# Four fused conv blocks on one core: image 0's input loaded once, late weights spread out, and two residual tiles of the last layer summed by GpSimd

## The chip, the core and the metric

The kernel runs on one core of a Trainium2 chip. The metric is the time of one execution on the device in microseconds (us). The engines are TensorE (PE; PEld is its weight load), VectorE (DVE), ScalarE (ACT), GpSimd (POOL), and SyncE (SP), which here only issues DMAs. Each engine works through its own queue in order and waits on semaphores.

## What is computed

Four images of 512 channels and 32 x 32 pixels go through four blocks, all in float32.

```python
# L0: 1x1 conv to 128, offsets by a 3x3 conv, deformable 3x3 conv, 1x1 conv to 512, residual
mid = relu(bn1(conv1x1(x)));  off = conv3x3(mid) + off_b
y = relu(bn2(einsum(w2, bilinear_gather(mid, off))))
x = relu(bn3(conv1x1(y)) + x)
# L1: correlation with the 5x5 neighbours, normalised, appended to the channels, 1x1 conv to 512
gs = l2norm(stack([sum_c(shift(x, dy, dx) * x) for dy, dx in 5x5]))
x = relu(einsum(W, concat([x, gs])) + b)
# L2, L3: 1x1 conv to 128, 3x3 conv, 1x1 conv to 512, residual
for layer in (2, 3):
    h = relu(s1 * conv1x1(x) + b1);  h = relu(s2 * conv3x3(h) + b2)
    x = relu(s3 * conv1x1(h) + b3 + x)
```

## The kernel before, in words

**The order.** `ORDER` (lines 44 to 200) is one list of some 1,550 items such as `ex.0.3.1.2`: kind, image, and further indices, mostly layer, half `h` of the pixels (512 columns each) and tile `m` of 128 channels. Each engine walks this list and carries out the items that are its own, so the list fixes every queue. It mixes the deformable conv of one image with L1 to L3 of the image before it. Five PSUM banks and a ring of four slots (`assign`, lines 246 to 269) are given out along the list; `take` (line 634) waits until the bank's last user has given it back.

**Start.** SP loads image 0's x into `xa` in eight parts of 256 KB (line 513), then seven weights (lines 514 to 517). ScalarE loads `w1` and the parameters `prm` (lines 828, 829), both counted by `ld_first`. PE runs three warm-up products on zeros (L653), waits for `ld_first` and runs conv1 (L666). ScalarE turns it into `mid`, PE makes the offset taps (L684), transposes (L674) and shifts (L694, L700), and VectorE computes the indices (`index`, L1071 to L1086). ScalarE writes image 0's pixels as a table to DRAM (`write_table`, L499, L501); later tables and the x of images 1 to 3 (`xload`, L507) are SP's.

**Gathers.** An image has 18 units (2 halves x 9 taps) of four gathers, 288 in all. GpSimd issues each as an indirect DMA (L597) and adds a small `tick` behind it (L602); in images 1 to 3 two memsets of `pause` follow each unit (L607). The gathers fill a ring of 12 slots; GpSimd waits for the blend of three units before. ScalarE weighs the first corner (`weigh`, L911), VectorE blends the other three (`blend`, L1189), PE transposes (`turn`, L730), ScalarE copies (`sampT`, L919), PE multiplies (`tap`, L741). After nine taps follow `hid`, `out0` (L749) and the residual sum `xsum` (L1194) with the tile of x that `res` loads into `x1` (L544). A value goes to PE as a high and a low part (fp32r); a product is then three matmuls (L630 to L632).

**The residual of L2 and L3.** It is added in one of two ways. Mostly PE adds it: `ex` starts with two matmuls of the identity with the high and low part of `xs` (L818), and then `exval` (layer 2) or `final` (layer 3: ScalarE at h = 0, L1007; VectorE at h = 1, L1257) applies bias and ReLU. Where `kept_sum` says so (before, only in image 3), GpSimd adds the two parts (`keep`, L613) into `kept`, which lies where `xs_low` lies, as soon as `red` has read them, `ex` is the three product matmuls alone, VectorE adds bank, bias and `kept` (`exsum` or `add`, L1250), and ScalarE applies ReLU (L1002).

The two ways stand in these lines:

```python
                elif kind == "ex":
                    _, i, layer, h, m = it
                    pe.wait_ge(cv_low, nth(("cvlow", i, layer, h)))
                    ...
                    alone = kept_sum(i, layer, m)
                    for p in range(0 if alone else 2):
                        pe.matmul(ps[:], ident_r[:], xs[p][:, m, h * HALF:(h + 1) * HALF], start=p == 0, stop=False)
```

Of the kernel before, what the change touches and what calls it, by code (L numbers as in the profile page):

```python
# [44 lines left out]
conv1.0.0 conv1.0.1 mid.0.0 taps.0.0 mid.0.1 taps.0.2 tapped.0.0 taps.0.1 tapped.0.2 midT.0.0 tapped.0.1 midT.0.1  # L45
pixels.0.0 shift.0 pixels.0.1 table.0.0 table.0.1 scale.0 scale.1 index.0 gather.0.0.0 hats.0 turnw.0 positions.0
turnw.1 split.1 gather.0.0.1 split.4 split.3 split.5 gather.0.1.0 weigh.0.0.0 splitlow.5 blend.0.0.0 gather.0.1.1
weigh.0.0.1 w3turn conv1.1.1 blend.0.0.1 xload.1.0 gather.0.2.0 weigh.0.1.0 gather.0.2.1 turn.0.0 xload.2.1 w3scale
gather.0.3.0 split.2 mid.1.1 split.0 splitlow.0 weigh.0.1.1 sampT.0.0 blend.0.1.0 conv1.1.0 gather.0.3.1 weigh.0.2.0
weigh.0.2.1 blend.0.1.1 gather.0.4.0 tap.0.0 mid.1.0 xload.2.0 midT.1.1 taps.1.1 taps.1.2 splitlow.1 midT.1.0  # L50
weigh.0.3.0 gather.0.4.1 blend.0.2.0 conv1.2.1 weigh.0.3.1 pixels.1.1 splitlow.3 splitlow.4 blend.0.2.1 gather.0.5.0
blend.0.3.0 xload.3.1 turn.0.1 sampT.0.1 tapped.1.1 tap.0.1 blend.0.3.1 gather.0.5.1 weigh.0.4.0 turn.0.2 taps.1.0
bias sampT.0.2 blend.0.4.0 conv1.2.0 tapped.1.2 mid.2.1 tapped.1.0 weigh.0.4.1 gather.0.6.0 blend.0.4.1 weigh.0.5.0
shift.1 gather.0.6.1 blend.0.5.0 mid.2.0 weigh.0.5.1 split.6 blend.0.5.1 gather.0.7.0 w3back turn.0.4 pixels.1.0 w3s
turn.0.3 index.1 midT.2.1 sampT.0.3 xload.3.0 gather.0.7.1 tap.0.2 pixels.2.1 weigh.0.6.0 taps.2.2 midT.2.0 turn.0.5
taps.2.1 corrw blend.0.6.0 splitlow.2 taps.2.0 gather.0.8.0 table.1.0 table.1.1 tap.0.3 sampT.0.5 weigh.0.6.1
pixels.2.0 conv1.3.1 res.0.0.1 blend.0.6.1 weigh.0.7.0 gather.0.8.1 tapped.2.0 weigh.0.7.1 blend.0.7.0 res.0.0.2
table.2.1 res.0.0.3 res.0.0.0 mid.3.1 gather.0.9.0 conv1.3.0 blend.0.7.1 sampT.0.4 weigh.0.8.0 gather.0.9.1 tap.0.4
turn.0.7 splitlow.6 blend.0.8.0 mid.3.0 tapped.2.1 weigh.0.8.1 midT.3.1 tap.0.5 gather.0.10.0 blend.0.8.1 midT.3.0
turn.0.6 pixels.3.0 sampT.0.6 tap.0.6 taps.3.1 weigh.0.9.0 turn.0.8 tapped.2.2 blend.0.9.0 gather.0.10.1 shift.2  # L60
weigh.0.9.1 hats.1 gather.0.11.0 sampT.0.8 blend.0.9.1 positions.1 sampT.0.7 weigh.0.10.0 tap.0.7 gather.0.11.1
tap.0.8 weigh.0.10.1 blend.0.10.0 index.2 gather.0.12.0 hid.0.0 blend.0.10.1 weigh.0.11.0 out0.0.0.0 out0.0.0.3
gather.0.12.1 blend.0.11.0 turn.0.9 weigh.0.11.1 hats.2 out0.0.0.2 sampT.0.9 pixels.3.1 xsum.0.0.0 res.0.1.0 table.3.1
blend.0.11.1 turn.0.11 taps.3.2 gather.0.13.0 weigh.0.12.0 turn.0.10 tapped.3.1 table.2.0 res.0.1.2 xsum.0.0.3
# [1247 lines left out]
```

## Time and profile before

| | us |
|---|---|
| median of 3 runs | 602.6 (602.46 to 603.48) |
| the profiled execution | 605.4 |
| its span | 603.6 |
| PE busy | 562.2 (93%) |
| POOL busy | 409.5 (68%) |
| DVE busy | 442.3 (73%) |
| ACT busy | 327.3 (54%) |

The page cuts the span into 40 slices of 15.1 us; a digit is the busy share of an engine in a slice in tenths. Lines of the profile name the engine, the line of the kernel, what is written from what, and how often. A chain of waits is followed back from the last instruction: at each step to what released it.

### The profile page before, as it was taken

The page shows a single profiled execution, that of the slowest core. Times are in us where ns is not written, and L with a number is a line of the kernel's source. Part 1 is how long each engine was busy: PE and PEld are TensorE (multiplying, and loading weights), DVE is VectorE, ACT ScalarE, POOL GpSimd, SP SyncE. Part 2 cuts the span into 40 slices and gives each one's busy share as a digit, 9 for nine tenths or more (in the row PEclk, how much of TensorE's full clock was granted, in tenths as well). Part 3 has the DMA queues.
Part 4 walks back from the last instruction along what each step waited for, and adds up shares of the span by engine and source line. Part 5 has one row for each costly group of instructions (what it writes and reads, how often), then busy time and mean ns, then how long its engine had stood idle before and what let it go on. Part 6 is the DMA issues. An engine that isn't in the chain of part 4 may idle for free.

```text
span 603.6 us, 8850 instructions
## 1 busy us (share of the span) xinstructions
PE 562.2 (93%) x2550; PEld 416.9 (69%) x2550; DVE 442.3 (73%) x1277; ACT 327.3 (54%) x718; POOL 409.5 (68%) x718
## 2 busy tenths in 40 slices
PE   9478986699999999799999999999999999999996
PEld 4434753576777777469777777688777776987774
DVE  3447789798988788689986788998884674463444
ACT  3445756446654874555645857654557633433534
POOL 2388888888888898888888888888787300003060
PEclk9888998899999999899999999999999999999999
DMA  8898997964568555866586557856765213000003
GB/s 307 286 355 292 276 366 222 310 186 143 160 193 296 165 150 162 280 205 171 168 264 204 168 168 251 251 159 175 223 183 148 72 59 134 0 1 1 1 1 139
DMA packets 48034, 110.08 MB, mean 182 GB/s; under 512 B 7655, under 2 KB 15911, under 8 KB 47858
## 3 DMA queue, kind: packets, MB, share of 16 engines
q0 software_dynamic: 23040, 75.52, 41.8%
q1 hardware_dynamic: 22274, 32.59, 15.6%
q10 hardware_dynamic: 2672, 1.41, 0.8%
q8 instruction: 21, 0.34, 0.3%
q14 instruction: 27, 0.22, 0.1%
HBM read 96.94 MB, written 12.55 MB: 181 GB/s over the span
## 4 chain that ended last, share of the span: by engine, by line
PE 71%; POOL 18%; DVE 4%; issue 3%; DMA 2%; ACT 1%; POOLq 0%; DVEq 0%; ACTq 0%
PE bank L630 16%; PE bank L632 16%; PE bank L631 16%; POOL patch L597 14%; PE bank L741 7%; POOL tick L602 4%; PE bank L749 4%; PE bank L818 4%; PE bank L730 4%; DMA patch<-patch_tables,idx_all 2%; PE bank L787 1%; PE bank L666 1%; PE bank L653 1%; DVE samp L1189 1%; DVE ring L1250 1%
## 5 line engine op out<-in xcount | busy, mean ns | idle before, releaser
L1189 DVE SCALAR_TENSOR_TENSOR samp<-patch,wgt_all,samp 128x128 f32<-128x128 f32 x864 | 240.7, 347 | 22.7 <-ACT samp L911 20.1
L597 POOL DMA_INDIRECT patch<-patch_tables,idx_all x216 | 219.8, 1017 | 40.2 <-DVE samp L1189 10.7
L911 ACT ACTIVATE samp<-patch,wgt_all 128x128 f32<-128x128 f32 x288 | 102.0, 396 | 76.4 <-DMA patch<-patch_table,idx_all 35.3
L597 POOL DMA_INDIRECT patch<-patch_table,idx_all x72 | 70.5, 980 | 30.9 <-DVE far L1086 20.3
L613 POOL TENSOR_TENSOR kept<-xs_high,xs_low 128x512 f32<-128x512 f32 x12 | 16.5, 1405 | 100.3 <-PE bank L632 100.3
L602 POOL TENSOR_TENSOR tick<-tick 1x1 f32<-1x1 f32 x288 | 79.7, 277 | 5.0
L741 PE MATMUL bank<-sampT,w 128*128 128x512 f32 x144 | 71.9, 606 | 1.5 <-ACT sampT L919 1.5
L730 PEld LDWEIGHTS bank<-ident_r,samp 128*128 128x128 f32 x288 | 35.8, 144 | 31.4 <-DVE samp L1189 16.8
L919 ACT ACTIVATE sampT<-bank 128x512 f32<-128x512 f32 x72 | 41.9, 591 | 27.8 <-PE bank L730 26.8
L730 PE MATMUL bank<-ident_r,samp 128*128 128x128 f32 x288 | 44.1, 280 | 10.5 <-DVE samp L1189 10.5
L630 PE MATMUL bank<-x_high,l1w_high 128*128 128x512 f32 x128 | 53.9, 421 | 0.0
L632 PE MATMUL bank<-x_high,l1w_low 128*128 128x512 f32 x128 | 50.2, 392 | 0.0
L631 PE MATMUL bank<-x_low,l1w_high 128*128 128x512 f32 x128 | 50.0, 391 | 0.0
L741 PEld LDWEIGHTS bank<-sampT,w 128*128 128x128 f32 x144 | 25.5, 193 | 17.4 <-issue 11.5
L630 PE MATMUL bank<-x_high 128*128 128x256 f32 x128 | 37.5, 293 | 0.0
L1230 DVE TENSOR_TENSOR h_low<-ring,h_high 128x512 fp32r<-128x512 f32 x16 | 12.1, 756 | 34.6 <-ACT h_high L983 34.6
L632 PE MATMUL bank<-x_high,x_low 128*128 128x256 f32 x128 | 36.2, 283 | 0.0
L631 PE MATMUL bank<-x_low,x_high 128*128 128x256 f32 x128 | 36.2, 283 | 0.0
L943 ACT ACTIVATE corr<-bank 32x320 f32<-32x320 f32 x64 | 27.3, 427 | 16.3 <-PE bank L632 14.0
L666 PE MATMUL bank<-xa,w 128*128 128x512 f32 x64 | 32.1, 651 | 2.6 <-DMA xa<-in_x 2.6
L749 PE MATMUL bank<-hid,w 128*128 128x512 f32 x64 | 31.7, 616 | 1.8 <-issue 1.8
L630 PE MATMUL bank<-hp_high,l2w_high 128*128 128x512 f32 x72 | 30.1, 418 | 0.0
(187 smaller groups left out, 1203.1 us busy)
## 6 DMA issues: line engine op xcount, KB each, us to landing
x_whole<-in_x SPq DMA_DIRECT2D x32, 256.0 KB, 7.2
out_y<-ring SPq DMA_DIRECT2D x32, 256.0 KB, 3.3
xa<-in_x SPq DMA_DIRECT2D x6, 1024.0 KB, 8.5
patch<-patch_tables,idx_all POOLq DMA_INDIRECT x216, 3.5
patch_tables<-midT SPq DMA_DIRECT2D x11, 256.0 KB, 7.1
xa<-in_x SPq DMA_DIRECT2D x8, 256.0 KB, 5.7
patch<-patch_table,idx_all POOLq DMA_INDIRECT x72, 6.0
l1w_whole<-in_l1wt SPq DMA_DIRECT2D x1, 1024.0 KB, 10.4
```

Of the source, the lines that this page charges most:

```text
L597: pool.indirect_dma_start(patch[:, n % SLOTS].rearrange("p a c -> p (a c)"), None, patches_n if i else patches_0, bass.IndirectOffsetOnAxi ...
L602: pool.tensor_tensor(tick[:, 1:2], tick[:, 0:1], tick[:, 0:1], ALU.add).then_inc(ticked, 1)
L630: pe.matmul(ps, w[0], a[0], start=start, stop=False)
L631: pe.matmul(ps, w[0], a[1], start=False, stop=False)
L632: return pe.matmul(ps, w[1], a[0], start=False, stop=stop)
L666: last = pe.matmul(ps[:], w1[:, c, :], xa[:, c, h * HALF:(h + 1) * HALF], start=c == 0, stop=c == KC - 1)
L730: last = pe.transpose(bank[TURN_BANK + u % 2][:, t * P:(t + 1) * P], samp[:, n % SAMPS, t, :], ident)
L741: pe.matmul(bank[TAP_BANK][:], w2[:, k, :], sampT[:, (UNITS * i + u) % SAMPS, :], start=k == 0, stop=k == TAPS - 1).then_inc(tap_done, 1)
L749: pe.matmul(ps[:], w3[:, m * P:(m + 1) * P], hid[:], start=True, stop=True).then_inc(out0_done, 1)
L911: act.activation(samp[:, n % SAMPS, t, :], patch[:, g % SLOTS, 0, :], ACT.Copy, scale=wgt_all[:, i, (HT * h + t) * TAPS + k, 0:1]).then_in ...
L919: act.activation(sampT[:, n % SAMPS, :], bank[TURN_BANK + u % 2][:], ACT.Copy).then_inc(sampT_done, 1)
L1189: dve.scalar_tensor_tensor(o_, g_, w_, o_, ALU.mult, ALU.add).then_inc(blended, 1)
```

## The change

- `kept_sum` also holds for tiles 2 and 3 of layer 3 in images 0 to 2: 12 `keep` and 12 `add` items more, and `mixhigh` of the next image waits for the `add` of its tile.
- Image 0's x is loaded once, as four whole chunks of 512 KB, straight into `x1`; conv1 of image 0 reads it there, chunk by chunk for both halves in turn, and the eight `res.0` loads are gone. x of image 1 is loaded right behind it, in two DMAs of two chunks each.
- The weights and the biases of L1 become ten items `ldw.n` of SP's queue. `ldw.8` (w2) and `ldw.9` (w3) wait for image 0's table, the others for a certain `turn` of image 0 (`WEIGHT_PACE`); x of images 2 and 3 waits for one too (`X_PACE`).
- Warm-up: one product and a half instead of three; conv1 waits for `w1` alone. VectorE computes its constants ahead of the batch-norm values.
- No pauses in image 1. Each image has a patch table of its own, so that the index needs no offset.
- `ORDER` is another one all through.

```diff
-PAUSE, PAUSES = 120, 2
+PAUSE, PAUSES = 120, (0, 0, 2, 2)
...
+WEIGHT_PACE = {7: 1, 2: 2, 3: 2, 4: 3, 5: 3, 0: 4, 1: 4, 6: 7}
+X_PACE = {2: 0, 3: 5}
...
+KEPT_OTHERS = ((3, 2), (3, 3))
...
 def kept_sum(i, layer, m):
 
-    return i == KEPT and (layer == 3 or m < KEPT_TILES)
+    return (layer == 3 or m < KEPT_TILES) if i == KEPT else (layer, m) in KEPT_OTHERS
...
             def load_x(i, h):
-                sp.dma_start(xa[:, :, h * HALF:(h + 1) * HALF],
-                             x_v[i, :, :, h * HALF:(h + 1) * HALF]).then_inc(ld_xa[h], 16)
-
+                some = slice(h * KC // 2, (h + 1) * KC // 2)
+                sp.dma_start(xa[:, some, :], x_v[i, :, some, :]).then_inc(ld_xa[h], 16)
+
+            for k in range(KC):
+                sp.dma_start(whole["x1"][:, k, PADK:PADK + H, :], grid_rows(x_v[0, :, k, :])).then_inc(ld_x0[k], 16)
             for h in range(2):
-                for k in range(KC):
-                    cols = slice(h * HALF, (h + 1) * HALF)
-                    sp.dma_start(xa[:, k, cols], x_v[0, :, k, cols]).then_inc(ld_x0[h][k], 16)
...
-                    sp.wait_ge(conv1_done, nth(("conv1", i - 1, h)))
+                    sp.wait_ge(conv1_done, nth(("conv1", i - 1, 0), ("conv1", i - 1, 1)))
+                    sp.wait_ge(turned, nth(("turn", 0, X_PACE[i] + h)))
                     load_x(i, h)
+                elif it[0] == "ldw":
+                    n = it[1]
+                    if n in WEIGHT_PACE:
+                        sp.wait_ge(turned, nth(("turn", 0, WEIGHT_PACE[n])))
+                    else:
+                        sp.wait_ge(tabled[0], table_dmas(0))
...
-                        for _ in range(PAUSES if i and t == HT - 1 else 0):
+                        for _ in range(PAUSES[i] if t == HT - 1 else 0):
...
-            for _ in range(3):
-                pe.matmul(bank[TURN_BANK][:], w3_s[:, 0:P], w3_s[:], start=True, stop=True)
-            pe.wait_ge(ld_first, 32)
+            for n in (C, C // 2):
+                pe.matmul(bank[TURN_BANK][:, 0:n], w3_s[:, 0:P], w3_s[:, 0:n], start=True, stop=True)
+            pe.wait_ge(ld_w1, 16)
...
+                        elif h == 0:
+                            pe.wait_ge(ld_x0[c], 16)
+                            for half in range(2 if c < KC - 1 else 1):
+                                last = pe.matmul(first[half][:], w1[:, c, :], residual(half, c),
+                                                 start=c == 0, stop=c == KC - 1)
+                        elif c == KC - 1:
+                            last = pe.matmul(first[1][:], w1[:, c, :], residual(1, c), start=False, stop=True)
...
+                    if i and kept_sum(i - 1, 3, m):
+                        act.wait_ge(add_done, nth(("add", i - 1, h, m)))
                     act.wait_ge(mix_done, nth(("mixB", i, h, m)))
```

## Rows read from the trace of the kernel before

**Rows 1.** The page: busy time, the 40 slices, and one group.
```profile
PE 562.2 (93%) x2550; PEld 416.9 (69%) x2550; DVE 442.3 (73%) x1277; ACT 327.3 (54%) x718; POOL 409.5 (68%) x718
...
PE   9478986699999999799999999999999999999996
...
L613 POOL TENSOR_TENSOR kept<-xs_high,xs_low 128x512 f32<-128x512 f32 x12 | 16.5, 1405 | 100.3 <-PE bank L632 100.3
```

**Rows 2.** The chain of waits: start us, us, what.
```profile
24.94 1.14 POOL patch L597
...
204.40 0.47 PE bank L818 x2
```

**Rows 3.** Stretches: busy us (x instructions) of each engine, granted clock, DMA share, GB/s.
```profile
22.00:135.00 113.00, 85.48 (x377) 56.89 (x376) 86.74 (x289) 61.18 (x147) 97.47 (x154) 0.89 0.88 287
257.00:580.00 323.00, 322.89 (x1507) 249.23 (x1507) 236.87 (x637) 175.45 (x382) 190.66 (x347) 1.00 0.47 140
...
253.50:256.70 3.20, 3.20 (x8) 1.61 (x7) 3.17 (x11) 2.52 (x8) 2.85 (x6) 0.50 0.81 232
```

**Rows 4.** Timeline, image 0's last gather and transposes: start us, us, what, idle before.
```profile
127.39 0.97 POOL L597 DMA_INDIRECT patch<-patch_table,idx_all  x1 [0.15 <-DVE samp L1189]
134.92 0.66 PE L730 MATMUL bank<-ident_r,samp 128*128 128x128 f32 x4 [0.61 <-DVE samp L1189]
```

**Rows 5.** Timeline and chain around 248 us.
```profile
243.63 0.97 POOL L597 DMA_INDIRECT patch<-patch_tables,idx_all  x1
250.91 0.43 POOL L607 MEMSET pause<- 1x120 f32 x2
251.50 1.03 POOL L597 DMA_INDIRECT patch<-patch_tables,idx_all  x1 [0.16 <-issue]
252.50 0.63 PE L730 MATMUL bank<-ident_r,samp 128*128 128x128 f32 x4 [4.22 <-DVE samp L1189]
254.21 1.06 PE L730 MATMUL bank<-ident_r,samp 128*128 128x128 f32 x4
243.63 7.25 DMA patch<-patch_tables,idx_all
```

**Rows 6.** Lines L818, L1250, L1002: ns min/median/max, first and last start.
```profile
L818 PE MATMUL bank<-xs_high,ident_r x52: 387/391/799, 201.5 to 572.0; 128*128 128x512 f32 x52
L1250 DVE SCALAR_TENSOR_TENSOR ring<-bank,prm,kept x8: 750/751/752, 590.8 to 599.7; 128x512 f32<-128x512 f32 x8
L1002 ACT ACTIVATE ring<-ring x8: 630/631/633, 591.5 to 600.5; 128x512 f32<-128x512 f32 x8
```

**Rows 7.** Timeline of the start, and image 0's loads (L513).
```profile
1.47 5.49 PE L653 MATMUL bank<-w_s 128*128 128x512 f32 x6 [1.47 <-DVE w_s L1024]
8.50 5.74 PE L666 MATMUL bank<-xa,w 128*128 128x512 f32 x13
14.08 2.74 PE L684 MATMUL bank<-offw,mid 128*128 128x162 f32 x16
DMA to landing us min/median/max: 3.5/5.7/6.6
```

**Rows 8.** Waits of PE (us in total, times, longest).
```profile
PE bank L715 <- DMA w<-in_w3t: 8.7, 1, 8.7
```

**Rows 9.** Timeline: last gathers and transposes of images 2 and 3.
```profile
354.94 0.96 POOL L597 DMA_INDIRECT patch<-patch_tables,idx_all  x1 [0.42 <-issue]
376.65 1.04 PE L730 MATMUL bank<-ident_r,samp 128*128 128x128 f32 x8
471.69 0.97 POOL L597 DMA_INDIRECT patch<-patch_tables,idx_all  x1
501.59 0.60 PE L730 MATMUL bank<-ident_r,samp 128*128 128x128 f32 x4
```

**Rows 10.** Timeline at 78 us.
```profile
78.47 2.38 POOL L602 TENSOR_TENSOR tick<-tick 1x1 f32<-1x1 f32 x1
78.52 2.29 DVE L1167 TENSOR_TENSOR l1w_low<-l1w_whole,l1w_high 128x2048 fp32r<-128x2048 f32 x1
```

More of the change, by code:

```diff
@@ L44 @@
 ORDER = """
[L45 to L64, printed above, removed]
@@ new lines @@
+pixels.0.1 shift.0 pixels.0.0 table.0.0 table.0.1 conv1.1.0 index.0 ldw.8 gather.0.0.0 mid.1.0 hats.0 midT.1.0 ldw.9
+positions.0 gather.0.0.1 gather.0.1.0 weigh.0.0.0 w3turn blend.0.0.0 conv1.1.1 gather.0.1.1 taps.1.0 gather.0.2.0
+mid.1.1 weigh.0.0.1 taps.1.1 tapped.1.0 blend.0.0.1 pixels.1.0 weigh.0.1.0 gather.0.2.1 blend.0.1.0 weigh.0.1.1
+tapped.1.1 blend.0.1.1 gather.0.3.0 w3scale weigh.0.2.0 turn.0.1 taps.1.2 blend.0.2.0 turn.0.0 gather.0.3.1 ldw.7
+xload.2.0 sampT.0.0 tapped.1.2 weigh.0.2.1 tap.0.0 xload.2.1 sampT.0.1 blend.0.2.1 gather.0.4.0 weigh.0.3.0 turn.0.2
@@ new lines @@
+blend.0.3.0 shift.1 ldw.2 gather.0.4.1 ldw.3 weigh.0.3.1 blend.0.3.1 gather.0.5.0 index.1 turn.0.3 weigh.0.4.0
+conv1.2.1 ldw.4 sampT.0.2 sampT.0.3 table.1.0 gather.0.5.1 blend.0.4.0 hats.1 ldw.5 midT.1.1 weigh.0.4.1 conv1.2.0
+positions.1 gather.0.6.0 split.3 blend.0.4.1 weigh.0.5.0 split.4 blend.0.5.0 gather.0.6.1 weigh.0.5.1 mid.2.1
+blend.0.5.1 mid.2.0 midT.2.1 gather.0.7.0 turn.0.4 tap.0.1 splitlow.3 ldw.0 weigh.0.6.0 taps.2.2 tap.0.2 blend.0.6.0
+ldw.1 gather.0.7.1 tap.0.3 sampT.0.4 tapped.2.2 weigh.0.6.1 taps.2.1 blend.0.6.1 midT.2.0 gather.0.8.0 scale.0
@@ new lines @@
+turn.0.6 weigh.0.7.0 xload.3.1 blend.0.7.0 pixels.1.1 turn.0.5 tap.0.4 sampT.0.6 taps.2.0 gather.0.8.1 pixels.2.0
+scale.1 tapped.2.1 table.2.0 sampT.0.5 turnw.1 split.2 w3back tapped.2.0 xload.3.0 turnw.0 gather.0.9.0 weigh.0.7.1
+shift.2 split.1 blend.0.7.1 weigh.0.8.0 pixels.2.1 blend.0.8.0 splitlow.4 gather.0.9.1 w3s weigh.0.8.1 turn.0.7
+tap.0.5 split.5 ldw.6 index.2 sampT.0.7 gather.0.10.0 table.2.1 conv1.3.0 weigh.0.9.0 bias gather.0.10.1 blend.0.8.1
+weigh.0.9.1 tap.0.6 split.0 blend.0.9.0 split.6 tap.0.7 gather.0.11.0 turn.0.8 weigh.0.10.0 sampT.0.8 splitlow.0
@@ L443, in lasts @@
         def lasts(it):
[L445 removed]
+            return len([f for f in ORDER if f[0] == "final" and kept_sum(f[1], 3, f[3]) and NTH[f] <= NTH[it]])
         def at_bank(it):
@@ L1252, in _ @@
                                              ALU.add).then_inc(exsum_done if layer == 2 else add_done, 1)
-                elif kind == "final" and it[1] < KEPT and it[2] == 1:
+                elif kind == "final" and not kept_sum(it[1], 3, it[3]) and it[2] == 1:
                     _, i, h, m = it
```

397 lines of the change are left out of this document (201 added, 196 removed).

## The prediction

> **What bounds the kernel now.** I read the page first. TensorE (PE) is busy for 562 us of the 603.6 us span, 93%, and in the 40 slices nearly all of what is missing lies in the first ten and in the last one [rows 1]. The chain of waits then tells two stages apart. From 24.94 us on it is a row of gathers on GpSimd (POOL) [rows 2], issues of 0.97 us each [rows 4] with a small `tick` behind; from about 165 us it is mostly matmuls. The table of stretches confirms it: from 22 to 135 us PE works 85.5 of 113 us and waits for samples, from 257 to 580 us it works 322.9 of 323 us [rows 3]. So the kernel is: a start that ends when image 0's indices are ready (24.94 us), a stage that GpSimd paces (72 gathers, to 128.4 us, one every 1.44 us [rows 2, 4]), and then whatever matmul work is left, with few holes.
>
> The hole that matters is one of 4.22 us: before the transposes that begin at 252.50 us [rows 5]. The chain names its cause: the last gather of image 1, issued at 243.63 us, needed 7.25 us to land; ScalarE stood at its weighing with the copy that PE's next transposes need queued behind it. PE's clock was granted at 0.50 just after that, from 253.5 to 256.7 us: its lower level, 1.2 GHz, after the idle [rows 3].
>
> **The change, part by part.** All is summed against the profiled execution (span 603.6, its own time 605.4 us). The median of the runs shown, 602.6 us, lies 2.8 us below the latter.
>
> *Identity matmuls, -5.6 us.* In image 0 to 2, layer 3, tiles 2 and 3, `ex` had two identity matmuls (L818) which add the residual. Now GpSimd sums the two parts (`keep`) and VectorE adds them (`add`). That is 3 images x 2 halves x 2 tiles x 2 = 24 matmuls. In the chain a pair takes 0.47 us [rows 2], though one is shown as 391 ns [rows 6], because they overlap; so 12 x 0.47 = 5.64 us. All 24 lie where PE has 20 of 20 us or nearly so; nothing hides them, and I take the whole. The new list of work has the same number of items of each kind on PE ahead of the last transposes of image 0 (`turn.0.17`, at 134.92 us [rows 4]); so what must follow that point is just these 5.6 us shorter.
>
> *What is added for them.* VectorE: 12 adds of 750 ns [rows 6] in place of its 6 `final`s of half 1; counting one of these alike, net 6 x 0.75 = 4.5 us. ScalarE: six ReLUs more, of 631 ns [rows 6], 3.8 us. GpSimd: 12 sums of 1.405 us [rows 1], 16.9 us. From 257 to 580 us VectorE is idle for 86 us, ScalarE for 148, GpSimd for 132 [rows 3]: the work itself is covered on average, and were it not, the sum would lose up to those amounts.
>
> *Pauses of image 1 removed.* Two memsets after each of 18 units. One pair holds the queue for 0.59 us (from 250.91 us to the next issue at 251.50 [rows 5]); 18 x 0.59 = 10.6 us of GpSimd's time. The gathers of image 1 end at 244.6 us now [rows 5]. After: -10.6, +1.4 for the one `keep` placed ahead of them, and the shift of the start below (+1.4): 236.8 us. PE wants the transposes of the last one, 254.2 us now [rows 5], at 254.2 - 4.2 - 1.7 + 1.4, less 1.5 of work that the new order puts behind them: 248 us, 11 us later. So the hole closes, -4.2 us, and with it the half-clock stretch: 3.4 us of matmuls at half speed, -1.7 us. The late landing fell together with image 0's stores; those now meet image 2's first gathers, with some 15 us to spare.
>
> *The start, +1.4 us.* Before, three warm-up products, six records, keep PE busy from 1.47 us for 5.49 us, 0.9 each, and conv1 follows without a break; its last 13 records take 5.74 us together, 0.44 each [rows 7]. Same shapes, twice the pace: the clock rose to its upper level in between. Now there are three records: 2.7 us, to 4.2 us; then PE waits for w1 and for the first whole chunk of x. Chunks are 512 KB now; before, eight of 256 KB landed 3.5 to 6.6 us after their issues [rows 7], which puts the first 512 KB near 6 us and all 2 MB near 10.8. So I expect conv1 to begin at the lower level. It has 16 records (two for each of 8 matmuls); I take six slow and ten fast: 6.0 + 6 x 0.87 + 10 x 0.43 = 15.5 us instead of 14.08 [rows 7], 1.4 later. Bounds: all fast and only the last chunk awaited, 10.8 + 4 x 0.43 = 12.5 us (-1.6); nine slow, 16.8 us (+2.7). I take the middle one, as the first products stayed at the slow pace for 5.5 us, and here there is a hole in their place. All behind it shifts: taps, shifts, index, first gather. The table of image 0 needs its second half first; its five DMAs, issued from 17.94 us, shift by half a us and stay hidden behind the index.
>
> *Image 0's x loaded once.* It drops eight loads of 256 KB around 76 to 105 us; no wait of PE is for such a load, so nothing is gained, and nothing lost. *Weights spread.* PE's wait of 8.7 us for w3 [rows 8] lies in the stage that GpSimd paces and is worth nothing. The weights now come when a certain transpose is done. SyncE waits for that, and queued behind it are x of images 2 and 3, the tables of images 1 to 3 and `bias`. The largest (L1's weights, 1 MB) is asked for after `turn.0.7`, near 82 us, with its split on ScalarE ahead of the weighing of unit 10, which was at 90.6 us; landing took 10.4 us in traffic. That can hold ScalarE for 0 to 3 us. GpSimd's ring of 12 gathers covers 3 us of it: 0.
>
> *New waits, +1.5 us.* `add` waits on VectorE for `keep`, with blends behind it; `keep` waits on GpSimd for `red`, with gathers behind it; `mixhigh` of the next image waits for `add`. Summing PE's work between the two in the written order, a `red` ends one to seven us ahead of its first `keep`, and `add.0.1.2` comes within 2 us of its `keep`, on which GpSimd has two sums to do (2.8 us). No row shows such a wait between images 0 and 2. Lower bound 0; upper 6 us, 1 for each of six places (two halves, three images). I take 1.5, nearer the lower end, because VectorE sits idle for a quarter of that stretch and can catch up. A gain is excluded: nothing is taken from these queues.
>
> **Sum.** -5.6 - 4.2 - 1.7 + 1.4 + 1.5 = -8.6 us; 605.4 - 8.6 = 596.8, less 2.8 to the median: 594.0 us. Its own range: 588 to 597.
>
> **Rivals.** (a) *The hole only moves.* With other order and tighter gathers, one of image 2's or 3's late landings stops PE instead, or the start costs 2.5 us and the new waits 4. For it: between the gathers' end and the transposes there are 9.6 us in image 1 (244.6 to 254.2), 20.8 in image 2 (355.9 to 376.7) [rows 5, 9]; the plan moves PE up at that second place by 8.8 us (4.2 + 1.7 + 4.3 of work put behind it - 1.4) and GpSimd by only 0.8 (10.6 - 1.4 - 6 x 1.4, for the six `keep`s ahead of it), leaving 13, of which landing, weighing and blending need some 7 to 10. Against: GpSimd rarely waits, so its time can be foretold. It gives 597 to 601.
>
> (b) *Slower: GpSimd's queue stands.* A `keep` waits for `red` with the gathers behind it. Eleven stand ahead of the last gather; if each holds the queue not 1.4 us but 3.3, that is 21 us more. By the above the gathers of image 3 end at 472.7 - 10.6 + 1.4 + 11 x 1.4 = 478.9 us; then at 499.9, and 10 us later, at 509.9, come the last transposes, 501.6 now, with 102 us behind them [rows 9]: 8.3 us more than now, 610.9 on the median. It decides only once these gathers end past 493 us, 14 us later than foretold; the 30 us from the last issue, 471.69 us, to the transposes [rows 9] speak against it.
>
> (c) *The port.* The trace shows the two engines blocking each other: the `tick` at 78.47 us took 2.38 us instead of 0.18, just as long as VectorE's two-input subtraction of 2.29 us beside it [rows 10]. Each `keep` may so hold VectorE for 1.4 us [rows 1]. All twelve on the path are 16.9 us: 594 + 16.9 - 1.5 = 609; half of them, 601. Against it stands VectorE's idle quarter [rows 3]. The Trainium skill (SBUF — State Buffer, "Who interferes with whom") speaks against this change: a VectorE instruction with two SBUF inputs and a GpSimd one that reads SBUF shut each other out for a whole instruction, and PE and ScalarE never wait so. By that rule, the trace agrees, in the `tick` above; the blends, most of VectorE's work, have two such inputs.
>
> **Chances.** Forecast 0.55 (588 to 597), (a) 0.25 (597 to 601), better than 588 0.06, (c) 0.09 (half of it on either side of the time before), (b) 0.05. A measurement of this kernel tells some 0.2%, 1.2 us. Faster by more 0.86, within 0.05, slower 0.09. Range 588 to 601.
>
> **What would show it.** L818 with 40 rather than 52 of each kind (104 to 80 in all); no hole of PE from 240 to 255 us; the first gather at 26.3 us (24.94 now); conv1's end near 15.5 us; the gathers of image 1 ended near 237 us; PE without waits for VectorE. Wrong: PE waiting for blends after 250 us (b, c), or a GpSimd wait for `red`; or a first gather past 28 us.

## The result, and the profile after

| | before | changed |
|---|---|---|
| median of its runs, us | 603.0 (602.5 to 605.9) | 609.1 (607.4 to 613.1) |
| profiled execution, us (its span) | 605.4 (603.6) | 607.4 (605.2) |
| ratio changed / before, 95% interval | | 1.0108 (1.0068 to 1.0148) |

The change makes the kernel 1.1% slower, some 6.5 us. A ratio leaves out single disturbed runs, those more than 1.5% above the fastest of their kernel; the medians hold all runs. The forecast was 594.0 us with a range of 588 to 601, so both the direction and the range were wrong. Of the rivals the one that came nearest is (c), the port: it said 609 if all twelve sums count. That its number fits so well is in part luck, as the last table shows.

The two profiled executions are only 2.0 us apart (605.4 and 607.4), as the changed one is among the fastest of its kernel and the other above its median. So the traces tell where time goes, and the ratios tell how much.

The page of the changed kernel, its busy times, the slices, and three groups of the costliest instructions:

```profile
PE 559.1 (92%) x2524; PEld 415.6 (69%) x2524; DVE 460.5 (76%) x1283; ACT 328.9 (54%) x724; POOL 422.3 (70%) x694
...
PE   8847858799999999799999999999999979999996
...
L1215 DVE SCALAR_TENSOR_TENSOR samp<-patch,wgt_all,samp 128x128 f32<-128x128 f32 x864 | 249.3, 356 | 29.9 <-ACT samp L935 27.3
...
L630 POOL TENSOR_TENSOR kept<-xs_high,xs_low 128x512 f32<-128x512 f32 x24 | 32.1, 1359 | 87.3 <-PE bank L649 87.3
...
L1256 DVE TENSOR_TENSOR h_low<-ring,h_high 128x512 fp32r<-128x512 f32 x16 | 14.4, 897 | 27.9 <-ACT h_high L1009 27.9
```

Beside [rows 1]: TensorE has 26 records (one record is one instruction in the trace) and 3.1 us of busy time less; the 24 products with the identity are among them. But it has two thin slices behind the start, the 17th and the 33rd, where the kernel before had one (the 17th). VectorE is busy for 18.2 us more, four times the 4.5 us of the prediction. GpSimd's sums (L613 before, L630 now) last as long as foretold, 1.36 us each. L1215 is the blend (L1189 before), and L1256 makes `h_low`, the low part of a hidden tile, for which TensorE's `ex` products wait (L1230 before).

The stretches, as in [rows 3]; busy us (x instructions) of PE, PEld, DVE, ACT, POOL, then granted clock, DMA share and GB/s. First the kernel before over 450 us, then the changed one over the same 450 us and behind each of its two large holes:

```profile
137.00:587.00 450.00, 443.31 (x2041) 338.21 (x2041) 337.72 (x927) 251.25 (x548) 303.42 (x542) 1.00 0.51 152
```

```profile
137.00:587.00 450.00, 438.91 (x2012) 334.86 (x2012) 355.16 (x935) 251.79 (x552) 316.12 (x518) 0.99 0.50 152
...
244.40:251.30 6.90, 5.84 (x18) 4.90 (x19) 4.73 (x16) 4.43 (x11) 6.23 (x10) 0.51 0.81 265
490.20:493.60 3.40, 3.40 (x12) 2.71 (x11) 3.24 (x9) 1.83 (x3) 0.00 (x0) 0.50 0.31 119
```

Before, TensorE stood for 6.7 of these 450 us; now for 11.1. Behind the first hole its clock is granted at half, 1.2 GHz, for 6.9 us, in place of 3.2 us before [rows 3], and behind the second for 3.4 us. The waits of TensorE by what they were for (us in total, times, longest), changed kernel:

```profile
PE bank L647 <- DVE h_low L1256: 6.7, 3, 3.9
...
PE bank L754 <- ACT sampT L943: 3.2, 1, 3.2
```

And the timeline of the two holes (start us, us, what, idle before it and its releaser), first around 242 us and then at 485 us:

```profile
245.46 1.09 PE L754 MATMUL bank<-ident_r,samp 128*128 128x128 f32 x4 [3.16 <-ACT sampT L943]
```

```profile
488.92 0.51 PE L647 MATMUL bank<-h_high,l3w_high 128*128 128x512 f32 x1 [3.94 <-DVE h_low L1256]
```

The hole of 4.22 us at 252.50 us [rows 5] did not close; it became a hole of 3.16 us seven us earlier. The second is new. What made it is in the next views. GpSimd's sums just ahead of it, then VectorE's blends there, and one of these blends by itself:

```profile
478.33 3.77 POOL L630 TENSOR_TENSOR kept<-xs_high,xs_low 128x512 f32<-128x512 f32 x3
```

```profile
476.60 5.99 DVE L1215 SCALAR_TENSOR_TENSOR samp<-patch,wgt_all,samp 128x128 f32<-128x128 f32 x6
```

```profile
477.71 4.54 DVE L1215 SCALAR_TENSOR_TENSOR samp<-patch,wgt_all,samp 128x128 f32<-128x128 f32 x1
```

All 864 blends at their line (duration in ns, min/median/max), changed kernel and then before:

```profile
L1215 DVE SCALAR_TENSOR_TENSOR samp<-patch,wgt_all,samp x864: 334/346/4543, 28.8 to 501.1; 128x128 f32<-128x128 f32 x173
```

```profile
L1189 DVE SCALAR_TENSOR_TENSOR samp<-patch,wgt_all,samp x864: 331/346/403, 33.2 to 499.2; 128x128 f32<-128x128 f32 x173
```

Six blends take 5.99 us beside three sums of 3.77 together. One of them lasted 4.54 us, 13 times the median, and ended at 482.25, just behind the last sum (482.10); of 864 before none was over 0.41. At 371 us it is an `h_low`, 0.69 us long by the median, beside two sums (GpSimd, then VectorE):

```profile
371.54 2.48 POOL L630 TENSOR_TENSOR kept<-xs_high,xs_low 128x512 f32<-128x512 f32 x2
```

```profile
371.66 2.92 DVE L1256 TENSOR_TENSOR h_low<-ring,h_high 128x512 fp32r<-128x512 f32 x1 [0.52 <-ACT h_high L1009]
```

The other end of the chain at 485 us is the `h_low` of image 2's last stage, which stands behind those blends on VectorE, and for which TensorE waits from 484.98 to 488.92 us.

### The profile page after: what moved, and what is told of

Its sections match the earlier page's. It is cut to its first block, busy times and chain, and to the rows that moved or that the text cites. A ratio compares the mean times of both kernels' runs of the same rounds, so it can differ in the third digit from the quotient of the medians.

```text
span 605.2 us, 8790 instructions
## 1 busy us (share of the span) xinstructions
PE 559.1 (92%) x2524; PEld 415.6 (69%) x2524; DVE 460.5 (76%) x1283; ACT 328.9 (54%) x724; POOL 422.3 (70%) x694
## 3 DMA queue, kind: packets, MB, share of 16 engines
q1 hardware_dynamic: 18978, 30.46, 14.2%
## 4 chain that ended last, share of the span: by engine, by line
PE 61%; POOL 19%; DVE 8%; issue 5%; DMA 3%; ACT 3%; DVEq 0%; ACTq 0%
POOL patch L614 15%; PE bank L647 14%; PE bank L649 14%; PE bank L648 14%; PE bank L765 6%; POOL tick L619 4%; DVE samp L1215 3%; PE bank L773 3%; PE bank L754 3%; DMA patch<-patch_table,idx_all 3%; PE bank L842 2%; PE bank L688 1%; PE bank L718 1%; PE bank L811 1%; DVE h_low L1256 1%
## 5 line engine op out<-in xcount | busy, mean ns | idle before, releaser
L614 POOL DMA_INDIRECT patch<-patch_table,idx_all x288 | 289.7, 1006 | 72.4 <-DVE far L1112 20.1
L1215 DVE SCALAR_TENSOR_TENSOR samp<-patch,wgt_all,samp 128x128 f32<-128x128 f32 x864 | 249.3, 356 | 29.9 <-ACT samp L935 27.3
L935 ACT ACTIVATE samp<-patch,wgt_all 128x128 f32<-128x128 f32 x288 | 100.2, 395 | 54.9 <-DMA patch<-patch_table,idx_all 50.2
L630 POOL TENSOR_TENSOR kept<-xs_high,xs_low 128x512 f32<-128x512 f32 x24 | 32.1, 1359 | 87.3 <-PE bank L649 87.3
L619 POOL TENSOR_TENSOR tick<-tick 1x1 f32<-1x1 f32 x288 | 83.5, 290 | 4.9
L765 PE MATMUL bank<-sampT,w 128*128 128x512 f32 x144 | 70.2, 596 | 2.8 <-ACT sampT L943 2.8
L1256 DVE TENSOR_TENSOR h_low<-ring,h_high 128x512 fp32r<-128x512 f32 x16 | 14.4, 897 | 27.9 <-ACT h_high L1009 27.9
L647 PE MATMUL bank<-hp_high,l3w_high 128*128 128x512 f32 x72 | 31.2, 433 | 0.3 <-DVE hp_low L1251 0.3
L954 ACT ACTIVATE x_high<-x_whole 128x512 fp32r<-128x512 f32 x32 | 19.7, 625 | 20.7 <-DVE x_whole L1220 20.5
L985 ACT ACTIVATE xs_high<-bank 128x512 fp32r<-128x512 f32 x32 | 17.7, 599 | 23.9 <-PE bank L811 23.9
```

Of the source, the lines that this page charges most:

```text
L614: pool.indirect_dma_start(patch[:, n % SLOTS].rearrange("p a c -> p (a c)"), None, tables[i].ap()[0:HW - W], bass.IndirectOffsetOnAxis(ap= ...
L619: pool.tensor_tensor(tick[:, 1:2], tick[:, 0:1], tick[:, 0:1], ALU.add).then_inc(ticked, 1)
L630: pool.tensor_tensor(kept[:, m, cols], xs[0][:, m, cols].bitcast(fp32), xs[1][:, m, cols].bitcast(fp32), ALU.add).then_inc(keep_done, 1)
L647: pe.matmul(ps, w[0], a[0], start=start, stop=False)
L765: pe.matmul(bank[TAP_BANK][:], w2[:, k, :], sampT[:, (UNITS * i + u) % SAMPS, :], start=k == 0, stop=k == TAPS - 1).then_inc(tap_done, 1)
L935: act.activation(samp[:, n % SAMPS, t, :], patch[:, g % SLOTS, 0, :], ACT.Copy, scale=wgt_all[:, i, (HT * h + t) * TAPS + k, 0:1]).then_in ...
```

## The experiments

The theories. **Port**: a sum that reads its two inputs from SBUF holds VectorE's two-input operation for as long as it lasts, and that is most of the loss. **Queue**: it is GpSimd's time for the sums, and their place among the gathers, whatever they do. **Order and pauses**: dropping the pauses or the new order is what hurts. Ratios are to the kernel before on the same chip, with the 95% interval; 0.1% is 0.6 us. A difference of two ratios has an interval of its own, some 2 to 4 us to either side; it stands in the table at the end. In the diffs `...` marks what is left out.

### Without the sums

```diff
-KEPT_OTHERS = ((3, 2), (3, 3))
+KEPT_OTHERS = ()
...
-keep.0.3.0.3 add.0.0.3 keep.0.3.0.2 add.0.0.2
```

> The changed kernel without its 12 new sums on GpSimd and 12 adds on VectorE: TensorE adds the residual of tiles 2 and 3 in images 0 to 2 again with 24 identity matmuls; order, loads and pauses stay as changed. Theory A (the sums cost more than they save: they hold VectorE by the shared port, and the adds hold VectorE's queue): TensorE gets 5.6 us more work but the holes at 237 to 245, 373 and 485 us (9.0 us in all, and 4 to 5 us of low clock behind them) shrink; about 604 us, at or below the changed kernel's 609. Rival B (the new order and the dropped pauses are at fault, the sums are a plain gain): about 609 + 5.6 = 614 us, with the hole near 240 us still there.

Measured: 602.1 us, 0.9963 (0.9926 to 1.0000). So the sums, adds and 24 dropped products together cost 1.45%, 8.7 us, where -5.6 with 1.5 for new waits had been foretold; all the rest of the change together is a gain of 0.4% (0 to 0.7%). The hole at 485 us is gone: of the waits for `h_low`, 6.7 us with the sums, this is left (L1253 is L1256 here).

```profile
PE bank L644 <- DVE h_low L1253: 1.6, 1, 1.6
```

The hole at 242 us is not gone, it is 2.4 us long: it is not made by the sums.

### Sums that read nothing

```diff
 pool.wait_ge(red_done, nth(("red", i, layer, h)))
+if i < KEPT:
+    for _ in range(3):
+        if pauses[0]:
+            pool.wait_ge(paused, pauses[0])
+        pool.memset(pause[:], 0.0).then_inc(paused, 1)
+        pauses[0] += 1
+    pool.memset(kept[:, m, cols], 0.0).then_inc(keep_done, 1)
+    continue
 pool.tensor_tensor(kept[:, m, cols], ...
```

> The changed kernel with each of the 12 new sums replaced by GpSimd work of about the same length that reads nothing from SBUF: three chained pauses and one memset of the same 128x512 tile; the residual of these tiles is thereby left out. Queues and waits stay as they are, only what GpSimd reads changes. Theory A1 (the port: a sum and a two-input VectorE instruction shut each other out): the blend that took some 4 us beside three sums at 478 us takes 0.35 us, and the hole of 3.94 us before the expansion at 485 us goes; 604 to 606 us. Rival A2 (waits in the queues alone: VectorE's add waits for a sum that stands behind gathers): no change, 609 us, hole of 3.9 us at 485 us still there.

The residual of these twelve tiles is left out here. Measured: 602.0 us, 0.9981 (0.9948 to 1.0015); its twin with true sums, the changed kernel, 1.0108 (1.0068 to 1.0148). The intervals don't touch; the difference is 1.27%, 7.7 us, and the time is below the 604 to 606 expected of the port. A stand-in beside the blends (GpSimd, then VectorE, then all blends of this kernel):

```profile
352.75 0.68 POOL L634 MEMSET pause<- 1x120 f32 x3
353.38 0.52 POOL L636 MEMSET kept<- 128x512 f32 x1
```

```profile
351.86 3.10 DVE L1223 SCALAR_TENSOR_TENSOR samp<-patch,wgt_all,samp 128x128 f32<-128x128 f32 x11
```

```profile
L1223 DVE SCALAR_TENSOR_TENSOR samp<-patch,wgt_all,samp x864: 334/346/405, 29.5 to 498.1; 128x128 f32<-128x128 f32 x173
```

Eleven blends follow one another every 0.28 us while GpSimd writes, and none of the 864 is over 0.41 us. In the changed kernel I took every VectorE instruction that overlaps one of the twelve sums and subtracted the median of its line: VectorE was held for 12.0 us in all, beside 12 x 1.35 = 16.2 us of sums. Here the same reckoning over the twelve writes gives nothing (under 0.1 us). A stand-in is 1.1 us long and a sum 1.35, so up to 3 us of GpSimd's time are in the 7.7 too; by the short stand-ins below (3.8 us of loss for 7 us of queue) I estimate 1.6 us for them. The port is the rest, some 6 us, with about 3 us of uncertainty.

### The sums and adds alone, in the order of before

```diff
-    return i == KEPT and (layer == 3 or m < KEPT_TILES)
+    return (layer == 3 or m < KEPT_TILES) if i == KEPT else (layer, m) in ((3, 2), (3, 3))
...
-gather.1.14.1 red.0.3.1 sampT.1.11
+gather.1.14.1 keep.0.3.0.2 red.0.3.1 sampT.1.11
```

> The kernel before, in its own order, with only the residual change put in: the same 12 sums, each placed alone behind one of the gathers that follow its reduction (for image 2 behind the last gather), and 12 adds just ahead of their final. If the sums themselves are a gain when they are not bunched and not late: 603 - 5.6 = 597 us. If they cost through the port wherever they stand: 601 to 605 us, with VectorE's busy time up by 8 us or more.

Measured: 612.9 us, 1.0166 (1.0112 to 1.0219), more than either expectation. The sums lose 10 us without the new order, the new start or the dropped pauses. Here four of them stand ahead of image 1's last gathers, and TensorE waits for an `h_low` (L1235) at 237 us:

```profile
241.84 0.65 PE L633 MATMUL bank<-h_high,l3w_high 128*128 128x512 f32 x1 [4.68 <-DVE h_low L1235]
```

### The changed kernel with image 1's pauses back

```diff
-PAUSE, PAUSES = 120, (0, 0, 2, 2)
+PAUSE, PAUSES = 120, (0, 2, 2, 2)
```

> The changed kernel with the two pauses after each unit of image 1 put back. Theory C (GpSimd in image 1 waits for the ring of 12 slots anyway, 5.6 us at 163 us, so the dropped pauses bought nothing): 609 us within 1.5 us, the gathers of image 1 end at 245 to 249 us. Rival (the pauses' 10.6 us are a gain that something else ate): 612 us or more, the gathers of image 1 end past 252 us.

Measured: 615.1 us, 1.0211 (1.0152 to 1.0270), 6.2 us slower than without them. The gathers of image 1 end at 249.4 us in place of 245.0. Dropping the pauses is a gain in the changed kernel too, so that part of the third theory is out.

### Before, without image 1's pauses

```diff
-                        for _ in range(PAUSES if i and t == HT - 1 else 0):
+                        for _ in range(PAUSES if i > 1 and t == HT - 1 else 0):
```

> The kernel before with the two pauses behind every second gather left out in image 1 only; nothing else changed. The prediction took 10.6 us of GpSimd time for them and the hole of TensorE at 248.3 to 252.5 us with the half clock behind it (4.2 + 1.7 us) as their price. If the pauses alone hold the hole open: 597 to 598 us. If GpSimd then only waits for the blends to free slots, as it did 5.6 us at 163 us in the changed kernel: the gathers of image 1 end 4 to 6 us earlier instead of 10.6, and the time is 598 to 601. If the pauses kept something else in order (gathers of small packets beside VectorE's work): 603 or more.

Measured: 597.9 us, 0.9927 (0.9894 to 0.9960). With this one line the kernel is faster than both others, by 4.4 us and 11 us. Its stretches, and image 1's last gather:

```profile
137.00:587.00 450.00, 448.45 (x2073) 343.18 (x2072) 340.75 (x931) 253.53 (x552) 299.85 (x508) 1.00 0.51 154
...
241.00:256.00 15.00, 15.00 (x60) 9.13 (x59) 13.27 (x38) 8.91 (x20) 13.21 (x25) 1.00 0.87 279
...
237.51 0.97 POOL L597 DMA_INDIRECT patch<-patch_tables,idx_all  x1
```

TensorE stands for 1.6 us of the 450, and in the 15 us around the old hole it doesn't stand at all. The last gather ends at 238.5 us where it was 244.6: 6.1 us of the 10.6 us of pauses, but enough. The hole and the slow clock were worth 5.9 us in the prediction; measured 4.4 (interval 2.4 to 6.4).

### No pauses at all

```diff
-                        for _ in range(PAUSES if i and t == HT - 1 else 0):
+                        for _ in range(0):
```

> The kernel before with no pauses at all. Without those of image 1 it took 597.9 us, and its trace shows no idle time of TensorE over 0.3 us between 137 and 587 us. If TensorE's own work sets the end from there: 597 to 599, the pauses of images 2 and 3 are worth nothing. If the blends and products of images 2 and 3 still run behind late gathers: 594 to 596. If gathers that run ahead take VectorE's time in the mixing: 600 or more.

Measured: 598.1 us, 0.9945 (0.9914 to 0.9976): the same as with those of images 2 and 3. TensorE no longer waited there (1.6 us of 450 above), and earlier gathers brought nothing.

### New start, old order behind it, no sums

```diff
-... weigh.1.0.0 gather.1.1.0 ...      (the new order from image 1's third gather on)
+... weigh.1.0.0 gather.1.1.0 ...      (the order of before from there on)
```

> The changed kernel without the sums (602.0 us) up to image 1's third gather, and from there the order of the kernel before, still without image 1's pauses. It differs from the kernel before without those pauses (597.9) only in the start (image 0's x once, weights spread) and the order of image 0. If the new order of image 1's blends ate the gain of the pauses: 597 to 599. If the new start costs the 1.4 us foretold, and more on the way: 600 to 602.

Measured: 599.2 us, 0.9947 (0.9921 to 0.9973). Against the kernel before without image 1's pauses that is +0.2%, 1.2 us, for the new start and image 0's order; against the changed kernel without sums -0.16%, 1.0 us, for the order from image 1 on. Either difference is less than its uncertainty. The traces do show what the order from image 1 on does to the gathers. GpSimd in the changed kernel at 162 us, and in the kernel before without the pauses at the same point:

```profile
161.73 0.97 POOL L614 DMA_INDIRECT patch<-patch_table,idx_all  x1
162.71 0.19 POOL L619 TENSOR_TENSOR tick<-tick 1x1 f32<-1x1 f32 x1
168.45 0.96 POOL L614 DMA_INDIRECT patch<-patch_table,idx_all  x1 [5.55 <-DVE samp L1215]
```

```profile
161.59 0.97 POOL L597 DMA_INDIRECT patch<-patch_tables,idx_all  x1
162.57 0.18 POOL L602 TENSOR_TENSOR tick<-tick 1x1 f32<-1x1 f32 x1
162.91 1.02 POOL L597 DMA_INDIRECT patch<-patch_tables,idx_all  x1
```

The new order has `blend.1.2.1` behind image 0's mixing on VectorE. It ends at 168.2 us, 10.5 later than before, and GpSimd needs its slot: half of the 10.6 us that the pauses gave is gone in one wait. The changed kernel without the sums has the same wait (5.5 us), so the sums don't make it; the kernel of this experiment has none over 1.3 us in image 1, and its gathers end 4.1 us earlier (242.4 against 246.4 us).

### One blend moved forward

```diff
-mixA.0.1.1 weigh.1.4.0 ... mixB.0.0.3 blend.1.2.1 corrT.0.1
+copies.0.3 blend.1.2.1 norm.0.0 weigh.1.3.0
```

> The changed kernel with one blend of image 1 (unit 2, second half) moved forward in VectorE's order, ahead of the norm of image 0's mixing, as it stood before the change; GpSimd waited 5.6 us for it at 163 to 168.5 us. Theory of the order: the gathers of image 1 end 4 to 5 us earlier than 245.0, the hole of TensorE at 242.3 (3.2 us) and the half clock behind it (6.8 us at half speed, some 3 us lost) go: 603 to 605 us. Theory of the port alone (the sums hold VectorE, and that is all the loss): the gathers come earlier, VectorE is late anyway: 608 to 610.

Measured: 610.3 us, 1.0112 (1.0073 to 1.0151): no gain. The blend now ends at 155.7 us, but GpSimd waits all the same, two gathers later:

```profile
169.95 0.96 POOL L614 DMA_INDIRECT patch<-patch_table,idx_all  x1 [5.16 <-DVE samp L1215]
```

This gather needs the slot of the next blend that is late, `blend.1.3.0`. The gathers of image 1 end at 242.9 us in place of 245.0, and 1.9 of these 2.1 us are there from the first gather on (22.9 us in place of 24.8). The new order has VectorE's work for image 0's mixing ahead of more than one blend, and to move one cures nothing.

### The sums spread out

```diff
-gather.3.17.0 ... keep.2.3.1.3 ... keep.2.3.1.2 ... keep.2.3.0.2 ... gather.3.17.1 ... keep.2.3.0.3
+gather.3.16.1 keep.2.3.0.3 ... gather.3.17.0 keep.2.3.0.2 ... gather.3.17.1 keep.2.3.1.3 ... keep.2.3.1.2
```

> The changed kernel with five of the twelve sums moved in GpSimd's queue and nothing else: image 0's second one from behind image 1's last gather to five gathers earlier; of image 2's four, which stood three together between two gathers, one behind each of two gathers before, and two behind the last. The number of sums is the same. Theory of the place: the waits for late sums (4.0 us at 246 us on VectorE) and the hole at 485 us (3.9 us and the half clock behind it, 1.7 us) go: 603 to 605 us. Theory of the port: every sum still holds a two-input operation of VectorE as long as it lasts, 12 x 1.36 us, wherever it stands: 607 to 610.

Image 0's `keep.0.3.0.2` also moves, from behind image 1's last gather to behind `gather.1.15.0`. Measured: 605.1 us, 1.0050 (1.0014 to 1.0086), 3.5 us better than the changed kernel (the two intervals overlap a little). TensorE's waits for `h_low`, as above 6.7 us with 3.9 the longest:

```profile
PE bank L647 <- DVE h_low L1256: 2.9, 3, 1.6
```

The new hole at 485 us is down to 0.7 us. VectorE is held for 8.7 us in place of 12.0. At the two last sums, in this kernel, it was GpSimd that stood: 3.75 us rather than 2.5.

```profile
486.85 3.75 POOL L630 TENSOR_TENSOR kept<-xs_high,xs_low 128x512 f32<-128x512 f32 x2
```

So the place of the sums matters, and they still lose: the kernel is 0.9% (5.2 us) above the one without them.

### No sums, no pauses, the blend moved

```diff
-PAUSE, PAUSES = 120, (0, 0, 2, 2)
+PAUSE, PAUSES = 120, (0, 0, 0, 0)
-KEPT_OTHERS = ((3, 2), (3, 3))
+KEPT_OTHERS = ()
```

> The changed kernel without the twelve new sums and adds (their 24 products with the identity are back), without any pauses in images 2 and 3 too, and with the one late blend of image 1 at its old place. Without the sums alone it took 602.0. If late gathers are what is left: the holes of TensorE at 242 us and after images 2 and 3 shrink: 595 to 599. If VectorE and the products set the time from there: 601 to 603, no faster than the kernel before.

The blend is moved as above. Measured: 601.4 us, 0.9993 (0.9961 to 1.0025), no better than without the sums alone (0.9963). The waits of GpSimd for blends, first without the sums alone, then here:

```profile
POOL patch L611 <- DVE samp L1212: 19.1, 21, 5.5
```

```profile
POOL patch L611 <- DVE samp L1212: 32.3, 22, 5.2
```

GpSimd waits 13.2 us longer for blends, in images 2 and 3, which lost their pauses: most of the 36 x 0.59 = 21 us that the pauses took comes back as waits.

### The sums in the order of before without image 1's pauses, and their stand-in

```diff
 # on top of "the sums and adds alone"
-                        for _ in range(PAUSES if i and t == HT - 1 else 0):
+                        for _ in range(PAUSES if i > 1 and t == HT - 1 else 0):
```

> The kernel before, its order kept, with two changes: image 1's pauses left out, and the twelve sums and adds in place of the 24 products with the identity, the sums one at a time behind gathers (image 2's beside their adds). With the pauses these sums made the kernel 9.5 us slower. If the sums cost what they hold VectorE up, wherever they stand: 605 to 608 us. If they cost only where gathers are late, and the pauses' 10.6 us of GpSimd time take up the twelve sums (16.3 us, 5.4 of them in image 1's gathers): 596 to 600.

Measured: 611.2 us, 1.0154 (1.0107 to 1.0201), 13.7 us (2.27%) above the same kernel without sums, and more than either expectation. The time freed by the pauses does not take up the sums. VectorE held by sums, measured as above: 13.7 us.

> The same kernel with each of the twelve sums replaced by three chained pauses and one write of zeros to the same tile: as long on GpSimd, but it reads nothing; the residual of these twelve tiles is left out. Theory of the port (a sum that reads two tiles holds VectorE's two-input operations): 598 to 600, some 7 us under its twin with the sums. Theory of the queue (the sums make later gathers late): the same time as its twin, 605 to 608.

Measured: 605.0 us, 1.0031 (1.0004 to 1.0058). The stand-in leaves out the residual of the twelve tiles, as above. Neither theory has it right alone: 7.4 us go with the reading, as in the changed kernel (7.7), and 6.3 us stay with stand-ins that read nothing, though 24 products are gone as well. In this pair the queue and the adds weigh nearly as much as the port.

### Short stand-ins

```diff
-                    for _ in range(3):   (the three chained pauses)
                     pool.memset(kept[:, m, cols], 0.0).then_inc(keep_done, 1)
```

> The changed kernel with each of the twelve sums replaced by a lone write of zeros to its tile (0.5 us of GpSimd in place of 1.36, and nothing is read; the residual of these twelve tiles is left out). With the same write behind three pauses (1.1 us) it took 602.0, and with no sums and all products with the identity 602.05. If the saving of the 24 products (5.6 us) was eaten by the time of the twelve sums in GpSimd's queue: 598 to 600. If it is eaten elsewhere, by the twelve adds on VectorE and the late gathers of image 1, which stay: 601 to 603.

The residual of the twelve tiles is left out here too. Measured: 599.0 us, 0.9918 (0.9885 to 0.9950). It differs from the 1.1 us stand-ins only by 12 x 0.6 = 7 us of GpSimd's queue: 0.63%, 3.8 us (1.0 to 6.6). So some half of that time in the queue reaches the end. And it is 2.7 us below the kernel without sums and with all 24 products (0.9963), half of the 5.6 us; the two intervals overlap, so that the exchange gains anything even with a sum that costs next to nothing is likely and not shown.

### Adding without GpSimd

```diff
-                    for p in range(0 if alone else 2):
+                    for p in ((0, 1) if not alone else (1,) if i < KEPT else ()):
                         pe.matmul(ps[:], ident_r[:], xs[p][:, m, h * HALF:(h + 1) * HALF], ...
...
-                                             kept[:, m, h * HALF:(h + 1) * HALF], ALU.add,
+                                             xs[0][:, m, h * HALF:(h + 1) * HALF].bitcast(fp32), ALU.add,
```

> The kernel before without image 1's pauses (597.9 us), and GpSimd sums nothing: in images 0 to 2, tiles 2 and 3 of the last layer, TensorE adds the low part of the residual by one product with the identity in place of two, and VectorE adds the high part straight from its tile. Twelve products less, some 2.8 us of TensorE; twelve adds of 0.75 us more on VectorE, six of its final steps of 0.7 us less. If TensorE's own work sets the end: 595 to 596. If the longer way of these tiles (product, add, final) makes TensorE wait: 598 to 600.

Measured: 601.0 us, 0.9960 (0.9933 to 0.9986), 2.0 us above its base (0.9927) where up to -2.8 was expected; the intervals overlap, so a gain of 2.8 us is ruled out and a loss not shown. TensorE's waits (total, times, longest) in this kernel:

```profile
PE bank L731 <- ACT sampT L921: 3.2, 2, 2.8
...
PE bank L631 <- DVE x_low L1205: 1.3, 1, 1.3
```

Neither wait is in its base. So without GpSimd's sums too, the longer way of these tiles makes TensorE wait; whether VectorE's twelve adds or ScalarE's six ReLUs more do it is not shown.

## Why the prediction was wrong, point by point

The parts, each as the difference of two measured ratios times 603 us, along one path of kernels from the one before to the changed one. Behind ± stands the 95% interval, estimated from those of the two ratios:

| part | foretold, us | measured, us |
|---|---|---|
| image 1's pauses dropped (the hole and half clock) | -5.9 | -4.4 ± 2.0 |
| new start and image 0's order | +1.4 | +1.2 ± 2.5 |
| order from image 1 on | 0 | +1.0 ± 2.7 |
| 24 products less, adds, sums of 0.5 us that read nothing | -5.6 + 1.5 | -2.7 ± 3.0 |
| sums 0.6 us longer, 7 us in GpSimd's queue | 0 | +3.8 ± 2.8 |
| sums that read SBUF (and last 0.25 us more) | 0 | +7.7 ± 3.1 |
| all | -8.6 | +6.6 |

Another path gives other parts: in the changed kernel the pauses are worth 6.2 us, and in the order of before the reading costs 7.4.

**"VectorE sits idle for a quarter of that stretch and can catch up."** This is the step that failed, with the chance of 0.09 that rested on it: the sums' hold on VectorE got no term in the sum, and the runs show +7.7 us (some 6 of it the port). The figure of 86 us idle [rows 3] was right, but it was a mean. Where blends and `h_low` stand in one order with TensorE behind them, a hold of 1 to 4 us goes through. The rival (c) had the mechanism, but its number is no confirmation: it has 16.9 us of hold all on the path, while VectorE was held for 12.0 us and 7.7 us reached the end; that 609 came out is luck, as 3.8 us in the queue, smaller gains than foretold and 1 us of the order make up the rest. It was held for unlikely because of that mean. The row for it, the `tick` of 2.38 us beside a subtraction of 2.29 [rows 10], was in the trace of before and showed the same lock in the other direction. I should have asked which blends stand beside each `keep` in the new order; the three `keep`s between `gather.3.17.0` and `gather.3.17.1`, at the end of image 3's gathers, would have stood out.

**The Trainium skill's rule** (SBUF — State Buffer, "Who interferes with whom") was right on both sides. A two-input VectorE instruction with both inputs in SBUF and a GpSimd one that reads SBUF exclude each other. The trace agrees: 0.35 us became 4.54. And it adds that a GpSimd instruction that only writes does not. The trace agrees here too: the twelve stand-ins didn't hold VectorE. That second half is the experiment that settled the case.

**"GpSimd rarely waits, so its time can be foretold."** Wrong, and the second step that failed. The gathers of image 1 were foretold to end at 236.8 us and ended at 245.0, with pauses dropped. 5.6 us went in one wait for `blend.1.2.1`. The kernel before without those pauses, in its old order, has them at 238.5. The prediction went through the new order of TensorE's items and of GpSimd's, but not through VectorE's, which frees the twelve slots.

**The sums' time in the queue** was put at 0 for the end, as covered. It is 3.8 us for 7 us (± 2.8). The sums stand among the last gathers of an image, which is where [rows 5] had shown the hole; those rows showed that GpSimd's time at this place is TensorE's time. Rival (a), the hole that only moves, was right that one stays, but not where: the old hole stays at image 1's end, and the new one at 485 us waits for VectorE and for no landing.

**Pauses**: right in mechanism; 4.4 us for 5.9. **Identity products**: TensorE's busy time is 560.0 us on the page without the sums and 556.4 with the short stand-ins, 3.6 us less for 5.6 foretold; and as soon as TensorE stands for other reasons, not all of it is gained (2.7 ± 3.0). **New waits**, 1.5 us: the one that came is VectorE's for `keep.0.3.0.2`, behind image 1's last gather though its `red` had long been done (idle before, and the keep):

```profile
246.50 0.75 DVE L1276 SCALAR_TENSOR_TENSOR ring<-bank,prm,kept 128x512 f32<-128x512 f32 x1 [3.99 <-issue]
```

```profile
245.15 1.25 POOL L630 TENSOR_TENSOR kept<-xs_high,xs_low 128x512 f32<-128x512 f32 x1
```

**The start**: conv1 did not end at 15.5 us. In the profiled run, TensorE and the first gather (before, conv1 ended at 14.24 and the first gather was at 24.94 us [rows 2, 7]):

```profile
4.91 8.26 PE L688 MATMUL bank<-x_whole,w 128*128 128x512 f32 x14 [0.51 <-DMA w<-in_w1t]
13.00 1.02 PE L691 MATMUL bank<-x_whole,w 128*128 128x512 f32 x2
```

```profile
24.79 1.14 POOL L614 DMA_INDIRECT patch<-patch_table,idx_all  x1 [20.15 <-DVE far L1112]
```

It began at 4.91 us, where 6.0 had been worked out from the landing of 256 KB chunks; its first records were slow, as foretold (last section), but five of them and not six. It ends at 14.0 us; in the other kernels with the new start at 12.1 to 15.3, and the first gather is at 22.9 to 26.1, against 13.7 to 14.2 and 24.4 to 24.9 in those with the old one. So 1.4 us was near the upper end of a term that is about half a us and varies more from run to run. **Image 0's x and the weights**, 0: no run tells them apart from the start. **Rival (b)**, the queue that stands, didn't occur: no wait for `red` appears in images 0 to 2.

What stays open: how the 6.3 us that the stand-ins cost in the old order divide between adds and queue; and the three parts of the table (+1.2, +1.0 and -2.7) that these runs can't tell from nothing.

## What to carry to other kernels

When work is moved to GpSimd, ask first whether it reads SBUF and which two-input VectorE operations stand beside it: here a memset cost VectorE nothing, sixteen microseconds of sums held it for twelve, and three sums back to back held one blend for all three. An idle share covers a delay only if no other engine waits for what stands right behind it: 27% idle covered neither the holds nor the queue. And before trading work between engines, take out what holds the gathers back: here one line with two pauses brought 4.4 us, and the exchange brought a loss.

## What the runs showed of the hardware

- Three sums back to back (3.77 us) held one blend for all three: it got no turn between them and lasted 4.54 us; the `h_low` at 371.66 us got none between two (2.92 us). The blend's record begins at 477.71 us, 0.6 us ahead of the first sum's, and still it was the blend that waited, so the recorded starts don't tell who will.
- The hold goes the other way too, in one place of this kernel: two sums took 3.46 us rather than 2.5, and the first of them beside two VectorE subtractions with both inputs in SBUF.

```profile
252.14 0.68 DVE L1227 SCALAR_TENSOR_TENSOR x_low<-x_whole,x_high 128x512 fp32r<-128x512 f32 x1
252.74 0.68 DVE L1256 TENSOR_TENSOR h_low<-ring,h_high 128x512 fp32r<-128x512 f32 x1
```

```profile
252.35 3.46 POOL L630 TENSOR_TENSOR kept<-xs_high,xs_low 128x512 f32<-128x512 f32 x2
```

- TensorE's products come at half the pace at first. In the changed kernel, with 2.93 us of warm-up, 0.51 us of waiting for weights, and conv1 behind, the first five records of conv1 take 0.8 us each, and the eleven behind them 0.43, from 8.9 us on (the columns are as in the stretches above; a record that crosses the border counts in both). The trace has no granted clock ahead of 8.93 us (before: 7.67), so the 1.00 of the first row says nothing, and it is the pace that tells the two levels apart.

```profile
4.90:8.90 4.00, 3.99 (x5) 1.86 (x6) 2.59 (x20) 1.17 (x1) 0.00 (x0) 1.00 1.02 384
8.90:14.00 5.10, 5.10 (x12) 1.90 (x10) 1.21 (x7) 1.05 (x3) 0.00 (x0) 1.00 0.93 378
```

- Before, with products from 1.47 us on and no break, conv1 is fast from 7.6 us on, not from the 8.50 us where the row of [rows 7] begins:

```profile
7.60 6.64 PE L666 MATMUL bank<-xa,w 128*128 128x512 f32 x15
```

- Where the upper level begins varies from run to run: in the seven traces with the old start at 4.8 to 7.7 us, in eight of the nine with the new one at 8.9 to 11.1, and in the ninth (one blend moved forward) at 5.0. In that one conv1 ends at 12.1 us, in the other eight at 14.0 to 15.3. That is why the start's term is no fixed number.
